# Raw images loaded in eighths, a second transform in half-precision pairs, weight products inside the modes stage, and a normalization divided over three engines

## The reference

```python
mean, var = over each (batch, group of 4 columns)            # 32 groups of the channel axis, all images of a batch
x = (x - mean) / sqrt(var + eps)                             # the first normalization
tokens_norm = instance_norm(x)                               # each image by its own mean and variance
k, q, v = spectral_conv(tokens_norm, w) + skip * tokens_norm + bias   # 1 -> 16 heads, lowest 16 x 9 modes of rfft2
prob = softmax(q @ k.T / scale)                              # per batch and head, 32 x 32
attn = prob @ v
x1 = instance_norm(spectral_conv(attn, proj) + skip + x)     # 16 heads -> 1, 32 x 17 modes
...                                                          # two spectral mixer layers with norms
...                                                          # an attention layer and an expert layer (best 2 of 8)
```

## Time and profile before

| what | value |
|---|---|
| median of 3 runs | 2462.3 us (2458.96 to 2466.84) |
| the profiled execution's own time | 2462.15 us |
| its span | 2460.4 us |
| mean granted TensorE clock | 0.901 |
| TensorE busy | 2118.0 us (86%) |
| VectorE busy | 1947.8 us (79%) |
| ScalarE busy | 1723.9 us (70%) |
| GpSimd busy | 616.5 us (25%) |

### The profile page before, as it was taken

One profiled execution on the slowest core, in us unless ns is written; L12 is line 12 of the kernel. 1 busy time (PEld: TensorE's weight loads), 2 busy tenths in 40 slices (PEclk: granted clock), 3 DMA queues, 4 the chain that ended last, 5 costly groups with the idle time before them and its releaser, 6 DMA issues. The chain is left out here.

```text
span 2460.4 us, 30994 instructions
## 1 busy us (share of the span) xinstructions
PE 2118.0 (86%) x10428; PEld 1091.7 (44%) x10428; DVE 1947.8 (79%) x3553; ACT 1723.9 (70%) x2471; POOL 616.5 (25%) x752
## 2 busy tenths in 40 slices
PE   7858573985589999999999999999999999756778
PEld 6823232772244444444444444444444444323332
DVE  4565797768878888888888888898888788667776
ACT  1254515646567888888888888888888888657676
POOL 0024620532540220220120121021000000036678
PEclk9978765555689999999999999999999999879999
DMA  9001436000000000000000000000000000000111
GB/s 296 1 1 69 129 86 146 1 1 1 6 1 1 1 1 1 1 1 1 1 1 1 1 1 1 1 1 1 1 1 1 1 1 1 9 13 22 31 31 44
DMA packets 80258, 55.73 MB, mean 23 GB/s; under 512 B 11220, under 2 KB 78676, under 8 KB 79077
## 3 DMA queue, kind: packets, MB, share of 16 engines
q1 hardware_dynamic: 74900, 52.38, 7.0%
q10 hardware_dynamic: 5200, 1.38, 0.3%
HBM read 36.91 MB, written 16.78 MB: 22 GB/s over the span
## 5 line engine op out<-in xcount | busy, mean ns | idle before, releaser
L1872 ACT ACTIVATE inner<-banks,key_bias,scales 128x1024 f32<-128x1024 f32 x512 | 617.2, 1206 | 211.1 <-PE banks L1745 205.9
L1994 DVE TENSOR_TENSOR weights_low<-weights,weights_high 128x1024 f16<-128x1024 f32 x512 | 675.5, 1319 | 17.0
L1879 ACT ACTIVATE weights<-inner 128x1024 f32<-128x1024 f32 x512 | 541.1, 1057 | 16.0 <-DVE weights_low L1994 0.3
L1990 DVE CAST weights_high<-weights 128x1024 f16<-128x1024 f32 x512 | 371.1, 725 | 180.9 <-ACT weights L1879 168.3
L2068 POOL CAST sums_high<-sums 128x512 f16<-128x512 f32 x32 | 39.4, 1231 | 1089.7 <-ACT sums L1862 1071.8
L1745 PE MATMUL banks<-queries_high,keys_high 128*128 128x512 f16 x1024 | 304.6, 379 | 0.7 <-ACT inner L1872 0.7
L1760 PE MATMUL banks<-weights_high,tokens_high 128*128 128x512 f16 x1024 | 304.6, 379 | 0.0
L1760 PE MATMUL banks<-weights_high,tokens_low 128*128 128x512 f16 x1024 | 304.5, 379 | 0.0
L1745 PE MATMUL banks<-queries_low,keys_high 128*128 128x512 f16 x1024 | 304.5, 379 | 0.0
L1760 PE MATMUL banks<-weights_low,tokens_high 128*128 128x512 f16 x1024 | 304.5, 379 | 0.0
L1745 PE MATMUL banks<-queries_high,keys_low 128*128 128x512 f16 x1024 | 304.5, 379 | 0.0
(11 more groups left out here) (569 smaller groups left out, 3387.3 us busy)
## 6 DMA issues: line engine op xcount, KB each, us to landing
images_b<-in_x SPq DMA_DIRECT2D x32, 256.0 KB, 6.7
images_a<-in_x SPq DMA_DIRECT2D x4, 2048.0 KB, 13.3
mixed_scratch<-images_a SPq DMA_DIRECT2D x4, 2048.0 KB, 6.3
result<-group_result SPq DMA_DIRECT2D x32, 256.0 KB, 2.3
images_b<-mixed_scratch SPq DMA_DIRECT2D x10, 768.0 KB, 5.0
images_a<-in_x SPq DMA_DIRECT2D x10, 768.0 KB, 9.3
mixer_weights<-in_L_conv_mixer_w SPq DMA_DIRECT2D x4, 272.0 KB, 6.3
table<-tables ACTq DMA_DIRECT2D x1, 772.5 KB, 5.9
```

The lines of the kernel that those rows point to most:

```text
L1872: act.activation(m.inner[:, t % 2, :], m.pair[t % 2], ACT.Exp, scale=m.fs[:, 1:2], bias=m.kb[:, c // QN % 2, k:k + 1]).then_inc(s.inner, 1)
L1879: act.activation(m.wt[:, t % 2, :], m.inner[:, t % 2, :], ACT.Exp).then_inc(s.outer, 1)
L1990: vec.tensor_copy(m.wH[:, t % DEEP, :], m.wt[:, t % 2, :]).then_inc(s.high, 1)
L1994: vec.tensor_tensor(m.wL[:, t % DEEP, :], m.wt[:, t % 2, :], m.wH[:, t % DEEP, :], ALU.subtract)\
```

## The change

- Memory: `dftH` and `dftL`, high and low half of the transform table times 128 in f16; `h33H` and `h33L`, the same of the scaled `half33` times 64, laid out like `half33`.
- Loads: behind every third group up to the 24th stands a load of an eighth of the raw images (8 of 1.05 MB in place of 4 of 2.1 MB); the statistics of a quarter wait for two of them.
- GpSimd splits the table at the start (three instructions of 66 elements).
- The two statistics matmuls stand behind groups 29 and 31; a square root of a table column ahead of ScalarE's copies loads the table; the first root stands behind copy 31, the second behind the scalings.
- ScalarE writes the scaled values as f16 high halves, and VectorE makes the low halves (scale and subtract in one instruction, chunk by chunk). TensorE multiplies three times for each k: high with high, high with low, low with high. ScalarE evicts the banks, with the factor 2^-13.
- Raw images: VectorE normalizes groups 0 to 7 behind its low halves, GpSimd groups 8 to 15 at the start of the modes stage, ScalarE groups 16 to 31 in the scores stage between its products and the exponential.
- The weight products move to VectorE's part of the modes stage, ahead of the Gram copy; the weights stage falls away.

```diff
         m.rstd, m.back = m.norms[3], m.norms[4]
+        m.dftH = sb(l0, "transform_high", [P, FQ], F16)[:, :]
+        m.dftL = sb(l0, "transform_low", [P, FQ], F16)[:, :]
...
+    m.h33H = b[:, 8448:8448 + P * K33].bitcast(F16).rearrange("p (t x) -> p t x", t=P)
+    m.h33L = m.spare[:, 0:P * K33].bitcast(F16).rearrange("p (t x) -> p t x", t=P)
+    m.scaled = m.mixw.rearrange("p r k c -> p (r k c)")[:, 2 * P:2 * P + FQ]
...
                 sp.dma_start(m.slots[:, g % SLOTS], cols[:, g * GRP:g * GRP + GRP, :]).then_inc(slot[g % SLOTS], 16)
-                if g in (3, 6, 9, 12):
-                    q = g // 3 - 1
+                if g % 3 == 2 and g < 24:
+                    r = slice(g // 3 * R, g // 3 * R + R)
+                    sp.dma_start(m.a[:, r, :], x[:, r, :]).then_inc(arrived[g // 6], 16)
 
...
         def _(pool):
             pool.memset(m.wraw, 0.0).then_inc(s.cleared, 1)
+            pool.wait_ge(s.dft, 16)
+            pool.tensor_scalar(m.scaled, m.dft, 128.0, None, ALU.mult).then_inc(s.split, 1)
+            pool.wait_ge(s.split, 1)
+            pool.tensor_copy(m.dftH, m.scaled).then_inc(s.split, 1)
+            pool.wait_ge(s.split, 2)
+            pool.tensor_tensor(m.dftL, m.scaled, m.dftH, ALU.subtract).then_inc(s.split, 1)
...
...
+            act.wait_ge(s.dft, 16)
+            act.activation(m.col[:, 12:13], m.dft[:, 0:1], ACT.Sqrt)
...
-                    if g == 28:
+                    if g == 31:
                         act.wait_ge(s.added, 1)
                         act.activation(rstd, var, ACT.Sqrt).then_inc(s.rooted, 1)
-                    if g == 30:
-                        act.wait_ge(s.added, 2)
-                        act.activation(m.col[:, 4:5], m.col[:, 3:4], ACT.Sqrt).then_inc(s.rooted, 1)
             act.wait_ge(s.fixed, 1)
             for lo, hi in chunks:
                 for b in range(NB):
                     t = slice(NT * b, NT * b + NT)
-                    e = act.activation(m.half33[:, t, lo:hi], m.half33[:, t, lo:hi], ACT.Copy, scale=m.col[:, 16 + b:17 + b])
+                    e = act.activation(m.h33H[:, t, lo:hi], m.half33[:, t, lo:hi], ACT.Copy,
+                                       scale=m.col[:, 16 + b:17 + b])
                 e.then_inc(s.high, 1)
+            act.wait_ge(s.added, 2)
+            act.activation(m.col[:, 4:5], m.col[:, 3:4], ACT.Sqrt).then_inc(s.rooted, 1)
             for r in range(rounds):
                 act.wait_ge(s.second, r + 1)
+                act.activation(m.ft[:, r * per:r * per + per, :].rearrange("p x y -> p (x y)"),
+                               m.ps[4 + r % 4][:, 0:per * FQ], ACT.Copy, scale=2.0 ** -13).then_inc(s.evicted, 1)
+            act.wait_ge(s.evicted, rounds)
-                if g == 25:
+                if g == 29:
                     pe.wait_ge(s.tables, 48)
                     pe.wait_ge(s.sums, 1)
                     pe.matmul(m.ps[4][:, 0:32], m.batch, total, start=True, stop=True).then_inc(s.averaged, 1)
-                if g == 27:
+                if g == 31:
                     pe.wait_ge(s.sums, 2)
...
+            pe.wait_ge(s.split, 3)
...
             for k in range(FQ):
                 r, j = divmod(k, per)
                 if k in begins:
-                    pe.wait_ge(s.high, begins.index(k) + 1)
+                    pe.wait_ge(s.low, begins.index(k) + 1)
                 if j == 0:
                     reached(pe, s.evicted, r - 3)
                 o = m.ps[4 + r % 4][:, j * FQ:j * FQ + FQ]
-                mm = pe.matmul(o, m.half33[:, :, k], m.dft, start=True, stop=True)
+                pe.matmul(o, m.h33H[:, :, k], m.dftH, start=True, stop=False)
+                pe.matmul(o, m.h33H[:, :, k], m.dftL, start=False, stop=False)
+                mm = pe.matmul(o, m.h33L[:, :, k], m.dftH, start=False, stop=True)
...
             for q in range(4):
-                vec.wait_ge(arrived[q], 16)
+                vec.wait_ge(arrived[q], 32)
                 for g in range(32):
...
-            vec.tensor_scalar(m.col[:, 16:20], m.ps[6][:, 0:NB], 1.0, None, ALU.mult)
+            vec.tensor_scalar(m.col[:, 16:20], m.ps[6][:, 0:NB], 64.0, None, ALU.mult)
...
+            for i, (lo, hi) in enumerate(chunks):
+                vec.wait_ge(s.high, i + 1)
+                for b in range(NB):
+                    t = slice(NT * b, NT * b + NT)
+                    e = vec.scalar_tensor_tensor(out=m.h33L[:, t, lo:hi], in0=m.half33[:, t, lo:hi],
+                                                 scalar=m.col[:, 16 + b:17 + b],
+                                                 in1=m.h33H[:, t, lo:hi],
+                                                 op0=ALU.mult, op1=ALU.subtract)
+                e.then_inc(s.low, 1)
+            vec.wait_ge(s.low, len(chunks))
+            for g in range(8):
+                vec.tensor_scalar(m.a[:, :, g * 4:g * 4 + 4], m.a[:, :, g * 4:g * 4 + 4],
+                                  mean[:, g:g + 1], rstd[:, g:g + 1], ALU.subtract, ALU.mult)
             vec.wait_ge(s.rooted, 2)
...
-            for g in range(16):
-                e = vec.tensor_scalar(m.a[:, :, g * 4:g * 4 + 4], m.a[:, :, g * 4:g * 4 + 4],
-                                      mean[:, g:g + 1], rstd[:, g:g + 1], ALU.subtract, ALU.mult)
-            c.step(e)
...
-            for r in range(rounds):
-                vec.wait_ge(s.second, r + 1)
-                vec.tensor_copy(m.ft[:, r * per:r * per + per, :].rearrange("p x y -> p (x y)"), m.ps[4 + r % 4][:, 0:per * FQ])\
-                    .then_inc(s.evicted, 1)
-            vec.wait_ge(s.evicted, rounds)
...
+            vec.wait_ge(s.copied, len(banks))
+            sk = m.skips
+            n5 = len(MT)
+            c.step(vec.tensor_tensor(w.sum, m.wT[:, :, 0, 0:48], over(sk[:, 0:48], 1, n5), ALU.add))
...
+            c.step(vec.tensor_tensor(m.dck, over(m.modesT[0:1, 0, 0, :], 1, HEADS), over(w.r2[0:1], 2, P), ALU.mult))
+            c.step(vec.tensor_tensor(m.dck, m.dck, over(w.r3[0:1], 2, P), ALU.add))
+            c.step(vec.memset(w.one[0:1], 1.0))
             vec.wait_ge(s.gram, 1)
             for b in range(NB):
...
+            for g in range(8, 16):
+                pool.tensor_scalar(m.a[:, :, g * 4:g * 4 + 4], m.a[:, :, g * 4:g * 4 + 4],
+                                   m.norms[1][:, g:g + 1], m.rstd[:, g:g + 1], ALU.subtract, ALU.mult)
             f = m.ft.rearrange("p (a x) (b y) -> p a x b y", a=2, b=2)
             for x in (0, 1):
...
-
-def stage_weights(nc, held, m):
-
-    s = semaphores(nc, held, "weights", "v")
-    w = weight_views(m)
-
-    with nc.Block() as block:
-        @block.scalar
-        def _(act):
-            for g in range(16, 32):
-                act.activation(m.a[:, :, g * 4:g * 4 + 4], m.a[:, :, g * 4:g * 4 + 4], ACT.Identity,
-                               bias=m.back[:, g:g + 1], scale=m.rstd[:, g:g + 1])
-
-        @block.vector
...
                 ins.then_inc(ready[3], 1)
+            for g in range(16, 32):
+                act.activation(m.a[:, :, g * 4:g * 4 + 4], m.a[:, :, g * 4:g * 4 + 4], ACT.Identity,
+                               bias=m.back[:, g:g + 1], scale=m.rstd[:, g:g + 1])
             act.wait_ge(s.sub, 1)
             act.activation(m.expo, m.score, ACT.Exp).then_inc(s.exp, 1)
...
             lambda: stage_modes(nc, held, m),
-            lambda: stage_weights(nc, held, m),
             lambda: stage_scores(nc, held, m),
...
         for i, stage in enumerate(stages[:upto]):
-            if i == 7:
+            if i == 6:
```

More of the change, by code:

```diff
@@ L331, in stage_tokens @@
     s = semaphores(nc, held, "tokens", "dft tables x0 x1 x2 x3 weights cleared scalars v sums averaged added rooted split "
-                                       "first copied spread picked fixed high second evicted")
+                                       "first copied spread picked fixed high low second evicted")
     slot = [nc.alloc_semaphore(f"tokens_slot_{i}") for i in range(SLOTS)]
@@ L623, in _ @@
-        @block.tensor
-        def _(pe):
-            for i, bank in enumerate(banks):
-                if i == 0:
-                    pe.wait_ge(s.weights, 1)
-                if bank[0][4] == 'modes':
-                    pe.wait_ge(s.modes, 1)
-                reached(pe, s.copied, i - NBK + 1)
-                for j, (src, n, _, wide, _) in enumerate(bank):
-                    mm = pe.transpose(m.ps[i % NBK][0:n, j * P:j * P + wide], src, m.ident[0:wide, 0:wide])
-                mm.then_inc(s.turned, 1)
-            pe.wait_ge(s.high, 1)
-            for r, cs in enumerate(hbanks):
-                i = len(banks) + r
-                reached(pe, s.copied, i - NBK + 1)
-                for j, k in enumerate(cs):
-                    mm = pe.transpose(m.ps[i % NBK][:, j * P:j * P + P], m.hg[:, k * P:k * P + P], m.ident)
-                mm.then_inc(s.turned, 1)
-            for k in range(HC):
-                pe.wait_ge(s.copied, len(banks) + k // 4 + 1)
```

(49 more changed lines are left out.)

36 lines of the change are left out of this document (6 added, 30 removed).

## The result

The changed kernel takes 2438.52 us (median of 4 runs, 2434.32 to 2438.81) against 2462.42: the ratio is 0.9899, interval 0.9882 to 0.9915. It is faster by 23.9 us, where 12.2 were forecast. The profiled execution is the fastest of the four (2434.32 us, span 2432.4 against 2460.4, 28.0 less), so stages are compared from their starts in the trace.

What follows compares the result with a forecast made beforehand. It took the first 200 us as barrier-separated stages, each set by the chain ending last. Terms -4.9 - 14.9 - 11.7 + 11.9 + 7.4 = -12.2 took 2462.2 to 2450 us; own range 2443 to 2458, with rivals 2434 to 2468.

Steps and rivals of the forecast that it cites:

- Loads: First transform: raw eighths shorten TensorE's wait, so it ends at 66.7 instead of 75.5 us.
- hand-over: From first transform's end to ScalarE's first scaling: a chain of 5.8 us, so scaling starts at 72.5, not 77.40: -4.9 us.
- second transform: Tokens stage: three f16 matmuls a k end at 18.6 us after scaling starts, against 33.5 before: -14.9 us.
- The strided load: Second transform's f16 weight loads: taken as hidden, 57 ns a matmul; upper bounds 122 and 243 ns.
- Weights stage gone, -11.7: Weight products, 11.1 us, fit VectorE's idle 13.3 us before the gram copy in the modes stage: -11.7 us.
- Blocking, +11.9: Modes stage: VectorE's chain waits out all eight GpSimd normalizations, 1.5 us each: +11.9 us.
- signs of being wrong: Modes stage: VectorE's chain as short as before, or GpSimd's operations beyond 2 us; also f16 matmuls above 100 ns apart.
- rival 1: Modes stage, no blocking: GpSimd's work runs beside VectorE's, 2438 us; chance 12%.
- Scores, +7.4: Scores stage: ScalarE's 16 affine operations, 11.39 us, delay the exponential from 188.66 to 196.0: +7.4 us.
- The bounds 0 and 23.8: Blocking price in the modes stage: 0 if GpSimd's eight slip beside VectorE, 23.8 us at twice the price.

Runs made afterwards that it cites:

- e5: Changed kernel with the second transform in f32 again, one matmul a k and no low halves on VectorE: 2454.73 us.
- e9: Kernel before with only the weight products merged into the modes stage, ScalarE's 16 normalizations in its gaps there: 2450.49 us, beside 2461.39 for before.
- e1: Changed kernel without GpSimd's eight normalizations in the modes stage (groups 8 to 15 stay raw): 2440.01 us.
- e7: Changed kernel with VectorE making all 16 normalizations of groups 0 to 15 in the tokens stage, GpSimd none in the modes stage: 2439.26 us.
- e2: Changed kernel with GpSimd's eight as two-input tensor_tensor instructions, mean subtracted, multiplication by rstd left out: 2446.71 us.
- e12: Changed kernel with GpSimd's eight as one one-input instruction of 4096 elements, runs of 32, constants: 2451.28 us, one execution.
- e14: Changed kernel with GpSimd's eight as one one-input instruction of 4096 elements, runs of 4, constants: 2446.94 us, one execution.
- e16: Changed kernel with GpSimd's eight as two one-input instructions of 2048 elements, runs of 32, constants: 2445.32 us, one execution.
- e3: Changed kernel with constants 0.5 and 2.0 for mean and rstd in GpSimd's eight (512 elements, runs of 4): 2443.58 us, one execution.
- e13: Changed kernel with GpSimd's eight of 512 elements in runs of 32 instead of 4, constants: 2436.25 us, one execution.
- e15: Changed kernel with GpSimd's eight as four one-input instructions of 1024 elements, runs of 32, constants: 2444.07 us, one execution.
- e4: Changed kernel with ScalarE's 16 normalizations moved from ahead of the exponential into its gaps in the modes stage: 2434.4 us.

## Why the prediction was half right

- *Loads*, *hand-over*, *second transform*: right, each within 0.9 us (66.7 against 67.37; the 5.8 from there to the scalings were 5.72; -14.9 was -14.3, and e5 gives 14.2). In the loads two errors nearly cancel: groups 3 to 5 started at 13.29, not 14.9, and TensorE's last wait ended at 53.23 ahead of group 24, not at 47.5 ahead of group 21.
- *The strided load*: 57 ns a matmul were 60, so the term held, and choosing by the nearest rows paid. "Hidden" was luck in part: it fits only at 1.2 GHz, for at 2.4 GHz the 60 ns stayed. The Trainium skill, "SBUF — State Buffer", The DMA port swizzle, says that each access that crosses to a new 16-byte line pays a penalty. The trace agrees in direction: the f16 elements lie 132 bytes apart (66 of 2 bytes), and such a load lasts 168 ns against 98. The term did not shrink by it, since 60 ns is little more than the 55 that the forecast had for 66 columns at the lower level.
- *Weights stage gone, -11.7*: right. e9 gives 10.9 by itself, and 11.15 from the start of the modes stage to that of the scores stage.
- *Blocking, +11.9*: the step that failed. "So I let VectorE's chain wait out every one of them" rested on one row, the 5.74 us of the earlier trace rows. That row is a two-input GpSimd instruction of 2048 elements; the eight are one-input ones of 512, beside which VectorE slips. What they add is 0.64 us in preparation and 2.9 in the weight products, and of that 0.2 to 1.0 us in the stage (e1, e7, e9), in place of 11.9. The size forecast for GpSimd itself was wrong too, 1.5 us where 2.1 to 4.2 were taken: with the lock held throughout, that would have been +20. Both of the signs of being wrong that the prediction named for this term came: VectorE's chain nearly as short as before, and GpSimd's operations beyond 2 us. The result is rival 1, at 2438, which had 12%; its price of nothing is nearly right, though the engines do collide, for 0.2 to 0.45 us at a time.
- The Trainium skill, "SBUF — State Buffer", Who interferes with whom, has the lock held for the whole instruction. e2, e12, e14 and the first instruction of e16 agree (a copy of 7.35 us beside 7.42). The changed kernel, e3, e13 and e15 do not: in the changed kernel three two-input instructions of VectorE in a row kept their 0.45 us beside one-input GpSimd instructions of 512 elements.
- *Scores, +7.4*: measured 5.6. The exponential came 6.2 later, not 7.4, counted from the stage's start (before it was 39.07 behind, now 45.23): the products had ended 1.2 us earlier in the stage. The other 0.6 lies between exponential and mixing, 10.96 us apart in place of 11.56; the granted clock rose ahead of the mixing (174.6) and not behind it as before (205.5), which was not tested as the cause. In e4, with the sixteen out of the way, the exponential comes 40.78 behind the stage's start, in e9 38.19, so most or all of the 6.2 is their place.

The profile allowed a smaller claim. It had no row of a short one-input GpSimd instruction beside VectorE. The bounds 0 and 23.8 were right to keep; the value was taken from the earlier trace rows, which differ from the case in both respects that turned out to decide, the number of inputs (e2, which changes the operation with it) and of elements (e12 to e16).

## What to carry to other kernels

A contention price belongs to the form of instruction it was measured on: before carrying it over, compare inputs and elements of both, and give the case "does not apply" the weight of a main case when both differ. Cut one-input GpSimd work (here f32 `tensor_scalar`, the only form tried) that must run beside a critical VectorE chain into pieces of at most 1024 elements a partition, and keep two-input work off GpSimd there: VectorE did twelve such products faster than eight beside GpSimd's four. Work moved off a stage of its own needs a gap that holds it: the sixteen normalizations fitted the modes stage, not the place ahead of the exponential. And before a difference of a microsecond between two stages with TensorE in them is read as an effect, compare where the granted clock rose in each.

## What the runs showed of the hardware that was not expected

- How long VectorE stands beside a one-input f32 GpSimd `tensor_scalar` jumps with its size: the same copy of 0.45 us takes 0.86 us at 512 elements (e13), 1.28 at 1024 (e15), 7.35 of GpSimd's 7.42 at 2048 (e16) and 14.26 of 14.33 at 4096 (e12). It was the same for runs of 4 and of 32 elements (e3 and e13, e14 and e12).
- It goes both ways: VectorE's 4356-element `tensor_scalar` (2.65 us) made the GpSimd instruction beside it last 4.24 us instead of 2.07 (changed kernel).
- An f16 weight load whose elements lie 132 bytes apart takes 168 ns in the median against 98 for adjacent ones, and the matmuls stay 60 ns apart when the granted clock doubles (changed kernel).
- Work ready 1.0 us earlier gave TensorE nothing in e1: the rise to 2.4 GHz came 6.0 us behind the first transpose there and 4.1 in the changed kernel. Over all runs it was 2.8 to 6.0.
